# Adding the output bias with TensorE: a three-part fp16 product in each output group instead of a GpSimd add on the residual

## The reference, cut to what matters

```python
x = x + attention(layernorm(x))        # attention ends in:  out @ Wo + bo
x = x + ffn(layernorm(x))              # ffn: shared experts + routed experts
```

## Time and profile before

| | |
|---|---|
| median of 3 runs | 2376.11 us (2374.84 to 2382.54) |
| time of the profiled execution | 2375.91 us |
| its span, first to last instruction | 2374.2 us |
| mean granted TensorE clock | 0.974 |
| busy: PE, ACT, DVE, POOL | 2172.2, 1634.9, 1532.0, 1119.2 us |
| L1193 on POOL (the bias) | 64 times, 1271 ns, 81.2 us busy |

### The profile page before, as it was taken

How to read it: one execution, slowest core, us unless ns; L and a number is a source line. 1 busy time by engine, 2 the same in 40 slices (tenths; PEclk the granted TensorE clock), 3 DMA queues, 4 the chain that set the end, 5 groups by cost and what they waited for, 6 DMA issues and landing times. The chain is left out here.

```text
span 2374.2 us, 42120 instructions
## 1 busy us (share of the span) xinstructions
PE 2172.2 (91%) x13868; PEld 1135.9 (48%) x13868; DVE 1532.0 (65%) x5008; ACT 1634.9 (69%) x4025; POOL 1119.2 (47%) x1558
## 2 busy tenths in 40 slices
PE   7678999999999999999999999999998886999997
PEld 3234444444444444444444444444443444666664
DVE  4645667676757666767676767676666654667764
ACT  5687676777777777676867677777676623666664
POOL 3224143444444444444444444444442635777885
PEclk9789999999999999999999999999999997999998
DMA  6022222222222222222222222222212025999996
GB/s 230 18 55 62 54 73 58 71 67 68 69 59 72 59 77 66 65 63 63 63 64 63 63 64 63 64 63 63 63 46 81 15 103 159 248 247 247 244 246 130
DMA packets 158362, 222.39 MB, mean 94 GB/s; under 512 B 37824, under 2 KB 91168, under 8 KB 158144
## 3 DMA queue, kind: packets, MB, share of 16 engines
q1 hardware_dynamic: 129472, 177.58, 25.0%
q0 software_dynamic: 28672, 42.12, 8.7%
HBM read 112.65 MB, written 56.46 MB: 71 GB/s over the span
## 5 line engine op out<-in xcount | busy, mean ns | idle before, releaser
L741 ACT ACTIVATE junk<-junk,nmax 128x512 f32<-128x512 f32 (+3 forms) x1024 | 573.7, 570 | 157.4 <-DVE nmax L1042 155.2
L1042 DVE CUSTOM_DVE_ANT_0 junk<-scores,maskrow 128x512 f32<-128x512 f32 (+3 forms) x1024 | 464.8, 486 | 209.2 <-PE scores L587 181.4
L731 ACT ACTIVATE probs<-scores_T 128x512 f32<-128x512 f32 x640 | 375.4, 604 | 44.9 <-PE scores_T L604 44.8
L1206 POOL TENSOR_SCALAR_AFFINE_SELECT probs<-probs 128x256 f32<-128x256 f32 x512 | 195.6, 417 | 349.2 <-ACT probs L731 348.9
L1214 POOL DMA_INDIRECT slots_dram<-rec,idx x256 | 263.2, 1028 | 115.7 <-issue 105.6
L587 PE MATMUL scores<-stack_k,stack_q 96*128 96x512 f16 (+3 forms) x1024 | 249.8, 305 | 44.0 <-DVE nmax L1042 43.9
L604 PE MATMUL scores_T<-stack_q,stack_k 97*128 97x512 f16 (+3 forms) x1024 | 248.5, 305 | 38.3 <-ACT probs L731 33.8
L741 ACT ACTIVATION_READ_ACCUMULATOR junk<-junk,nmax 128x1 f32 x1024 | 212.3, 207 | 0.0
L1193 POOL TENSOR_TENSOR xres<-xres,bo 128x512 f32<-128x512 f32 x64 | 81.2, 1271 | 258.7 <-DMA xres<-in_x 258.7
L213 PE MATMUL dense<-xT_hi,wqkv_hi 128*128 128x512 f16 x512 | 197.6, 386 | 1.5 <-DVE xT_lo L1013 1.5
L215 PE MATMUL dense<-xT_hi,wqkv_lo 128*128 128x512 f16 x512 | 196.3, 383 | 0.0
(11 more groups left out here) (276 smaller groups left out, 5489.3 us busy)
## 6 DMA issues: line engine op xcount, KB each, us to landing
stack_q<-split_q SPq DMA_DIRECT2D x384, 64.0 KB, 2.0
stack_k<-split_k SPq DMA_DIRECT2D x384, 64.0 KB, 2.1
out<-xres SPq DMA_DIRECT2D x67, 256.0 KB, 3.2
x2n<-in_x SPq DMA_DIRECT2D x64, 256.0 KB, 3.1
xres<-in_x SPq DMA_DIRECT2D x64, 256.0 KB, 3.0
x2n_dram<-x2n SPq DMA_DIRECT2D x16, 1024.0 KB, 4.3
stack_q<-in_W_gate SPq DMA_DIRECT2D x16, 512.0 KB, 3.7
stack_q<-in_W_up SPq DMA_DIRECT2D x16, 512.0 KB, 5.4
```

Source lines behind the costliest of these rows:

```text
L731: act.activation(to, at, ACT.Exp, scale=SCALE / (QS * QS)).then_inc(exp_done, 1)
L741: last = act.activation(x, x, ACT.Exp, scale=-1.0, bias=c["nmax"][:, hg % 2, m:m + 1], accum_out=c["sums"][:, hg % 2, m:m + 1])
L1042: last = dve.tensor_tensor_reduce(out=c["junk"][:, JUNK_AT[f], at:at + cols], in0=ps["scores"][f % 2][:, at:at + cols], in1=c["maskrow"][: ...
L1206: last = pool.affine_select(out=blk, in_=blk, compare_op=ALU.is_ge, fill=0.0, base=0, pattern=[[0, 2], [1, P]], channel_multiplier=-1)
```

## The change

POOL no longer adds the bias. DVE waits for the residual's load itself. Each output product begins with one more matmul into the same bank, of a constant `share` (96 x 128) with `brow` (96 x 512, fp16): rows 0 to 31 of `brow` hold the first fp16 part of the scaled bias, rows 32 to 63 the second, rows 64 to 95 the third, and the constant includes 1/32, since each part stands in 32 rows. The parts are made once, by DVE, in turn 0 at `BV_ADDED`, each instruction linked to the one before it by a semaphore; POOL fills `share` in the setup.

```diff
 HS = 2.0 ** 4
+BS = 2.0 ** 7
...
-        self.bias = {bias_pace * (t + 1): t for t in range(TT)}
...
             pool.memset(c["half"][:, :], -0.5)
+            pool.memset(c["share"][:, :], AS * WS / BS / HD)
...
                 if kind == "out":
                     if m == 0:
                         pe.wait_ge(aT_ready, s * HG + k + 1)
-                    last = product(pe, bank[:, :], both(c["aT"], ALL, k, blk), both(c["wo"], ALL, k, ALL), k == 0, k == DK - 1)
+                    if k == 0:
+
+                        pe.matmul(bank[:, :], c["share"][0:3 * HD, :], c["brow"][0:3 * HD, :], start=True, stop=False)
+                    last = product(pe, bank[:, :], both(c["aT"], ALL, k, blk), both(c["wo"], ALL, k, ALL), False, k == DK - 1)
...
                 if kind == "out":
                     x1 = c["xres"][:, m, :]
-                    dve.wait_ge(xres_biased, s * TT + m + 1)
+                    dve.wait_ge(xres_loaded[m], (s + 1) * 16)
...
                 if slot == BV_ADDED:
                     dve.wait_ge(bv_done, 1)
-                    dve.tensor_tensor(c["bo"][:, :], c["bo"][:, :], ps["o"][:, :], ALU.add).then_inc(bo_ready, 1)
+                    link(dve.tensor_tensor(c["bo"][:, :], c["bo"][:, :], ps["o"][:, :], ALU.add))
+
+                    rest, brow = c["att"], c["brow"]
+                    link(dve.tensor_scalar_mul(brow[:, :], c["bo"][:, :], BS))
+                    link(dve.scalar_tensor_tensor(rest[:, :], c["bo"][:, :], BS, brow[:, :], ALU.mult, ALU.subtract))
+                    link(dve.tensor_copy(brow[HD:2 * HD, :], rest[HD:2 * HD, :]))
+                    link(dve.tensor_copy(brow[2 * HD:3 * HD, :], rest[2 * HD:3 * HD, :]))
+                    link(dve.tensor_tensor(rest[2 * HD:3 * HD, :], rest[2 * HD:3 * HD, :], brow[2 * HD:3 * HD, :], ALU.subtract))
+                    dve.tensor_copy(brow[2 * HD:3 * HD, :], rest[2 * HD:3 * HD, :]).then_inc(bo_ready, 1)
...
-            def add_bias(s, t):
-                pool.wait_ge(xres_loaded[t], (s + 1) * 16)
-                if in_first(s) and t == 0:
-                    pool.wait_ge(bo_ready, 1)
-                xt = c["xres"][:, t, :]
-                pool.tensor_tensor(xt, xt, c["bo"][:, :], ALU.add).then_inc(xres_biased, 1)
-
...
-                    if fin and slot in plan.bias:
-                        add_bias(i - 2, plan.bias[slot])
...
+            c["share"], c["brow"] = sb("share", [P, P], F16), sb("brow", [P, D], F16)
```

More of the change, by code:

```diff
@@ L88, with __init__ @@
 class Plan:
-    def __init__(self, groups, slots, bias_pace, route_pace, route_now, route_late, scatters):
+    def __init__(self, groups, slots, route_pace, route_now, route_late, scatters):
         ends, at = {}, 0
@@ L105, in __init__ @@
         self.scatter = {slot: (m, n) for m, slots in scatters.items() for n, slot in enumerate(slots)}
[L108 to L111, removed]
+PLAN = Plan(GROUPS, 126, 1, ROUTE_NOW, range(1, 1 + 2 * (ROUTE_STEPS - ROUTE_NOW), 2), {0: range(61, 109, 3)})
+PLAN_1 = Plan(GROUPS_1, 126, 1, 0, (), {})
+PLAN_16 = Plan(GROUPS_16, 126, 1, ROUTE_STEPS, range(1, 1 + 2 * (ROUTE_STEPS - ROUTE_NOW), 2), {0: range(31, 63, 2), 1: range(74, 122, 3)})
+PLAN_17 = Plan(GROUPS_17, 0, 3, ROUTE_STEPS, (), {})
 def plan_of(i):
@@ L336, in sequences @@
         rstd1_ready, rstd2_ready = sem("rstd1_ready"), sem("rstd2_ready")
-        xres_biased, out_ready = sem("xres_biased"), sem("out_ready")
+        out_ready = sem("out_ready")
         sig_exp, sel_ready, dest_ready = sem("sig_exp"), sem("sel_ready"), sem("dest_ready")
```

## The result

The changed kernel takes 2344.0 us (median of 4 runs, 2342.3 to 2345.9); the kernel before took 2375.8 us on the same chip (4 runs). The ratio is 0.9872, with a 95% interval from 0.9846 to 0.9897: 31.8 us less, where 15.7 were forecast. The profiled execution went from 2375.91 to 2342.3 us, its span from 2374.2 to 2340.6, so the two traces have 33.6 us to account for.

What follows compares the result with a forecast made beforehand. TensorE was taken to set the pace, with a stall each turn behind POOL's queue. Products +13.9, stalls -26.8, turn 16 -6.2 and preparation +3.4 gave -15.7 us, so 2360 us, range 2350 to 2373.

Steps and rivals of the forecast that it cites:

- rival A: The forecast itself: the stall before the denominators goes, the products are paid; 2351 to 2366 us, chance 0.62.
- The chain: Turns 3 to 15: tile 3's add, behind its load, delays tile 0's scale, then ACT's exps and TensorE's denominators.
- the margin of 1 us: At the denominators: the last exp would end about 1 us before TensorE arrives, so the stall goes wholly.
- The products: TensorE's 64 added bias matmuls, each paid at 0.217 us between starts: +13.9 us.
- The preparation: Turn 0: six DVE instructions at `BV_ADDED`, paid in full as TensorE waits for DVE: +3.4 us, bounds 2.5 and 4.5.
- Does such a wait cost its full length? It does.: Stall before denominators: turn 9 against turn 7, 1.5 us more waiting gives 1.5 us more turn.
- the 26.8 us: TensorE's idle time before the denominators, together over turns 3 to 15, all taken as gain: -26.8 us.
- Turn 16: TensorE's waits of 1.91 and 4.32 us for exps, behind late loads and POOL, go: -6.2 us, bounds -2 and -9.
- DVE beside POOL: DVE instructions delayed while POOL's adds run, at most some 0.9 us a turn: taken as nothing, bound 3 us.

Runs made afterwards that it cites:

- The two versions with later adds: Kernel before, POOL's adds in later slots behind the scales, no products: with turn 17 also later 2349.9 us, ratio 0.9847; with turn 17 unchanged 2348.1 us, ratio 0.9826.
- The adds' last order: Kernel before, POOL's adds moved behind the scales in usual turns and turn 16, turn 17 unchanged, no products: 2348.1 us, ratio 0.9826.
- The kernel with one add moved: Kernel before, in usual turns the add of tile 3 moved from slot 12 to 14, behind the scale of tile 0: 2344.5 us, ratio 0.9870.
- the one with only the waits: Changed kernel, POOL waiting for the four residual loads in the old slots, with no add: 2354.3 us, ratio 0.9919.
- the waiting adds put back: Changed kernel plus useless adds on POOL in the old slots, behind the old wait for the residual's load: 2382.5 us, ratio 0.9979.
- the products put in: Kernel before, adds kept, plus 64 products of zeros on TensorE and no preparation on DVE: 2382.8 us, ratio 0.9979.
- the two kernels on chip C: Changed kernel with POOL's bare load waits, 2354.3 us; kernel before with the add of tile 3 moved to slot 14, 2344.5 us.

## Why the prediction was right in its mechanism and wrong in its size

The forecast was rival A's mechanism, and that came true in every turn; three terms of its sum were too small, and a part of the distance is luck. Against the steps as they stand there:

- **The chain** load, POOL, ACT, TensorE, with the add of tile 3 before the scale of tile 0: right. The stall went in all 13 turns, to the margin of 1 us that was forecast (turn 7: the last exp ends at 772.40, TensorE comes at 773.40). Taking the load's wait out of POOL's path does it alone, and moving that add by two slots does 23 of 28 us of it.
- **The products**, +13.9 us at 0.217: right, shown by taking them out. The distance of 131 ns that the Trainium skill gives for a sustained stream (TensorE: Matmul & The Clock Gate, Back-to-back issue gap) isn't seen here either: 217 ns.
- **The preparation**, +3.4: right in the rows. Its six instructions last 3.06 us together, and the links between them cost some 0.05 us each, where 0.07 was taken, for which no row stood. It doesn't show when the two starts are compared: up to turn 2's denominators 0.3 us were gained, where 3.4 and turn 2's products, 0.9, were to be lost. That is 4.5 us of the difference between forecast and profile. From the start of `value_bias`'s products, just before the preparation, to those denominators TensorE was at 1.2 GHz for 53.9 us before and for 47.8 after, which is 3.0 us of loss, and these products begin 1.3 us earlier. The change hasn't touched them. The two versions with later adds, which differ in turn 17 alone, differ in the same way (the products take 6.5 us before and 3.5 after, 3.5 and 6.5 in these two, and they reach turn 2's denominators at 196.3 and 201.7 us); so I put this down to chance.
- **"Does such a wait cost its full length? It does."** This is the step that failed: a wait costs more than its length. I compared a turn with a stall of 3.39 us with one of 1.87 and found that the difference of the stalls is the difference of the turns. What each stall costs beside its length cancels in that. The turn to compare with was turn 2, without a stall, in the view of the earlier trace rows:

```profile
195.59 0.69 DVE L1007 SCALAR_TENSOR_TENSOR xres<-dense,xres 128x512 f32<-128x512 f32 x1 [2.27 <-PE dense L215]
...
308.84 0.69 DVE L1007 SCALAR_TENSOR_TENSOR xres<-dense,xres 128x512 f32<-128x512 f32 x1 [0.41 <-PE dense L215]
```

  It takes 113.25 us. With 0.87 for the products that gives 114.1, and 114.1 to 114.6 is what a turn takes now; the twelve from 3 to 14 had averaged 115.9. The adds' last order, which has no stall and no products, shows the whole price: from turn 2's denominators to turn 15's it takes 1474.2 us, and the kernel before 1507.1. So the 13 stalls cost 32.9 us up to there, where 26.8 were in the sum. What they cost beside the 26.8 us:
  - Some 0.16 us each, 2.1 in all. The idle time is counted from the modelled end of the last matmul, 0.38 us after its start, while without a stall the next would start 0.217 after it. The rows of the kernel before, ahead of turn 14's denominators, show it: 1.74 us between starts, 1.52 more than 0.217, for an idle time of 1.36.

```profile
1591.67 0.38 PE L215 MATMUL dense<-wo_hi,aT_lo 128*128 128x512 f16 x1
1593.41 0.63 PE L624 MATMUL scores_T<-ident,att 128*128 128x128 f32 x4 [1.36 <-ACT probs L731]
```

  - Waits of 0.28 to 0.50 us at L604 just ahead of it in four turns, 1.4 us in all. I had left them out.
  - The clock: 1.7 us each behind two of the stalls, the second of them behind turn 15's denominators. All this is 6.9 us; the 5.2 of it that lie before that mark leave 0.9 of the 32.9 us unnamed.
- **Turn 16**, -6.2 us with -9 as a bound "if the low clock behind the long wait goes too": it went. Between the denominators of turns 15 and 16 the idle time fell from 9.1 to 3.9 us and the clock loss from 5.1 to nothing (1.7 of it the drop behind turn 15's stall), with 0.87 of products added: -9.4 from these, -9.3 measured. The low clock was in the range and not in the sum, and there for this turn alone: a term that was left at nothing, of which turn 16 itself measured 3.4 us.
- **DVE beside POOL**, priced at nothing with 3 us as the bound: 2.3 us of it were on the path, in turn 17. POOL's three adds at its start held a DVE instruction that TensorE waits for. Before, POOL, DVE and TensorE:

```profile
1904.12 3.73 POOL L1193 TENSOR_TENSOR xres<-xres,bo 128x512 f32<-128x512 f32 x3
```

```profile
1905.62 2.79 DVE L1079 TENSOR_TENSOR aT_lo<-att,aT_hi 128x512 f16<-128x512 f32 x1 [0.70 <-ACT aT_hi L756]
```

```profile
1908.46 0.61 PE L213 MATMUL dense<-wo_hi,aT_hi 128*128 128x512 f16 x1 [2.92 <-DVE aT_lo L1079]
```

The kernel with one add moved, whose adds stand there as before, shows 2.79 us again, the adds' last order, with the same slots in this turn, 1.43, and the one with only the waits 0.69. After, the same instruction takes 0.69 us and TensorE waits 0.61:

```profile
1874.05 0.69 DVE L1083 TENSOR_TENSOR aT_lo<-att,aT_hi 128x512 f16<-128x512 f32 x1 [0.69 <-ACT aT_hi L760]
```

```profile
1874.80 0.39 PE L213 MATMUL dense<-wo_hi,aT_hi 128*128 128x512 f16 x1 [0.61 <-DVE aT_lo L1083]
```

The 17.9 us between -15.7 and -33.6, then: the start 4.5; between the marks clock loss 6.8 and 3.5 beside the stalls' length, less 1.0 since turn 16's waits gave 5.2 and not 6.2; turn 17's contention 2.3. That is 16.1. Another 1.8 us I haven't traced: 0.7 between the marks and 1.1 in the rest of turn 16. The failed step stands for 6.9 us of it, turn 16's own clock for 3.4. The 4.5 of the start are luck; without them the profiled execution would have taken 2346.8 us, still below the low end of 2350.

What the runs leave open: that the clock falls because of the stall isn't shown one by one. What they show is that it goes with them. Between the marks the loss is 6.8 us in the kernel before, 5.1 with the waiting adds put back, and none in the five kernels in which POOL waits for no load (the changed one, the same again, without products, without the preparation, with the adds but not their wait); the kernels that kept a wait in turn 16 lost 1.7 or 3.4 us there. Against it: the longest stall of all, turn 9's 3.39 us, has full clock behind it, and so have the 13 stalls of 0.7 to 1.9 us with the products put in.

## What to carry to other kernels

An engine that does short steps for others in a fixed order should do those first, and work that waits for a load after them: its busy time says nothing of what its queue costs. Before work is moved to the engine that bounds the kernel, move it by a slot or two in its own queue; here that gave the whole gain, with nothing to pay on TensorE. To price a stall, compare with a turn that has none, and not two turns with stalls of different lengths.

## What the runs showed of the chip

- Behind stalls of about 2 us of TensorE the granted clock was 1.2 GHz for 3.4 us in 2 of 13 turns, and stayed at 2.4 GHz in the others, turn 9 with its 3.39 us among them; the loss of some 1.7 us is nearly as large as the stall.
- A two-input DVE instruction of 128x512 went from 0.69 to 2.79 us while three adds of POOL ran. The Trainium skill (SBUF — State Buffer, Who interferes with whom) says that a DVE instruction with two inputs in SBUF contends with a GpSimd one that reads SBUF, for a port pair that only one of them can hold. The trace agrees, and adds that one DVE instruction can be held through more than one POOL instruction that follow each other: it ended at 1908.41, 0.6 us after the third.
- Turn 16's tail, from its denominators to turn 17's first tile, took 83.3 us before and 80.1 after, 82.3 and 83.3 in the two kernels on chip C, and 92.8 to 94.7 us in all eight on the chips A and B. The changed kernel itself took 80.1 in one place and 92.8 on chip B. There some of TensorE's waits are put down to "issue", as this one in the last version of the adds' order:

```profile
1790.44 2.36 PE L613 MATMUL o_ps<-probs,v 128*32 128x512 f32 x32 [1.11 <-issue]
```

Why the chips differ stays open. So times are to be compared on one chip, and across chips by their ratios alone.
